# Two scans of a gated recurrence: which of a VectorE instruction's semaphore waits is named first

## The reference, cut to what matters

```
h1_new = tanh(h1 * (1 - alpha) + sigmoid(h1 @ Wh.T + z_t @ Wz.T + b) * z_t)
```

```
z  = sigmoid(xz_t + h @ U_z + vz)
r  = sigmoid(xr_t + h @ U_r + vr)
hh = tanh(xh_t + r * h @ U + vh)
h_new = (1.0 - z) * h + z * hh
```

## Time and profile before

| | |
|---|---|
| median of 3 runs | 3118.3 us (3117.98 to 3118.93) |
| profiled execution | 3121.06 us, its span 3119.7 us |
| busy in the span | PE 88%, PEld 71%, DVE 66%, ACT 52%, POOL 11% |
| stretch with layer 2's steps | 187 to 2283 us, 1024 steps, 2096 / 1024 = 2.05 us each |
| L1765 and L1747 | 1024 and 1023 instructions, 183 ns each |
| EVENT_SEMAPHORE L1764 | 1024, median 50 ns; L1746: 1023, 21 ns each |

### The profile page before, as it was taken

The page is one execution under the profiler, slowest core; times in us unless marked ns, Lnnn a source line. Parts: engine busy times, 40 slices in busy tenths (PEclk is TensorE's granted clock), DMA queues, the critical chain, the costliest instruction groups (busy, mean ns, idle before and its releaser), DMA issues.

```text
span 3119.7 us, 149803 instructions
## 1 busy us (share of the span) xinstructions
PE 2751.6 (88%) x59217; PEld 2221.1 (71%) x59220; DVE 2045.6 (66%) x12108; ACT 1609.6 (52%) x8443; POOL 341.2 (11%) x457
## 2 busy tenths in 40 slices
PE   7689899999999999899999989988659999979984
PEld 4478888888888888788888878877636666644331
DVE  6688888766776666766667665655447666666238
ACT  3445555566666666666666655543325555521115
POOL 0000101101010010100101001010114444410000
PEclk7555555555555555555555555555559999989997
DMA  3142323223122231222312220000457766242000
GB/s 126 41 122 79 96 70 93 62 64 92 49 84 75 66 103 49 83 71 72 94 59 83 63 79 17 4 17 5 170 188 241 218 194 198 86 146 84 0 0 27
DMA packets 170138, 270.88 MB, mean 87 GB/s; under 512 B 23353, under 2 KB 125644, under 8 KB 167140
## 3 DMA queue, kind: packets, MB, share of 16 engines
q1 hardware_dynamic: 125524, 202.29, 20.6%
q0 software_dynamic: 15312, 33.67, 3.2%
q10 hardware_dynamic: 28608, 25.35, 3.0%
HBM read 170.77 MB, written 98.70 MB: 86 GB/s over the span
## 4 chain that ended last, share of the span: by engine, by line
PE 77%; DVE 10%; ACT 5%; issue 5%; DMA 1%; DVEq 1%; SPq 0%; POOL 0%; POOLq 0%; ACTq 0%
PE bank_h L676 7%; PE bank_h L685 7%; PE bank_z L676 7%; PE bank_r L676 6%; PE work L676 6%; PE bank_g L676 5%; PE work L666 5%; PE bank_r L685 3%; DVE h_run L1765 3%; PE bank_z L685 3%; ACT hh_run L1208 3%; PE work L898 3%; PE bank_z L898 3%; PE work L923 2%; PE bank_g L685 2%
## 5 line engine op out<-in xcount | busy, mean ns | idle before, releaser
L676 PEld LDWEIGHTS work<-h_run,hi_r 128*128 128x128 f16 x4092 | 212.7, 109 | 323.6 <-DVE h_run L1765 312.9
L676 PE MATMUL work<-h_run,hi_r 128*128 128x2 f16 x4092 | 277.7, 172 | 169.7 <-DVE h_run L1765 162.7
L1765 DVE TENSOR_TENSOR_SCAN h_run<-z_run,hh_run 128x12 f16<-128x12 f32 x1024 | 187.1, 183 | 326.1 <-ACT hh_run L1208 281.4
L1208 ACT ACTIVATE hh_run<-bank_h 128x4 f32<-128x4 f32 x1024 | 180.1, 176 | 349.2 <-PE bank_h L685 348.9
L1747 DVE TENSOR_TENSOR_SCAN rh_run<-r_run,h_run 128x12 f16<-128x12 f32 x1023 | 186.9, 183 | 213.1 <-ACT r_run L1198 198.7
L1189 ACT ACTIVATE r_guess<-work 128x4 f32<-128x4 f32 x1023 | 177.0, 173 | 286.1 <-PE work L676 274.0
L676 PE MATMUL bank_g<-h_hi,hi_g 128*128 128x2 f16 x4092 | 253.0, 166 | 38.8 <-ACT h_hi L1178 37.0
L685 PE MATMUL bank_h<-rh_run,hi_h 128*128 128x2 f16 x4092 | 270.9, 170 | 10.2 <-DVE rh_run L1747 3.7
L676 PE MATMUL bank_h<-h_run,hi_h 128*128 128x2 f16 x4092 | 256.8, 167 | 3.2 <-DVE h_run L1744 0.5
L685 PE MATMUL bank_g<-h_lo,hi_g 128*128 128x2 f16 x4092 | 252.7, 166 | 4.3 <-issue 2.8
L685 PE MATMUL bank_r<-h_run,hi_r 128*128 128x2 f16 x4092 | 251.5, 165 | 2.4 <-DVE h_run L1781 0.5
(11 more groups left out here) (481 smaller groups left out, 7780.4 us busy)
## 6 DMA issues: line engine op xcount, KB each, us to landing
stage<-in_gate_up SPq DMA_DIRECT2D x128, 384.0 KB, 3.7
stage<-in_down SPq DMA_DIRECT2D x128, 192.0 KB
gu_split<-parts SPq DMA_DIRECT2D x64, 384.0 KB, 2.7
gu_ring<-gu_split SPq DMA_DIRECT2D x64, 384.0 KB
xt<-x_rows ACTq DMA_DIRECT2D x191, 128.5 KB, 2.2
x_rows<-zero_rows SPq DMA_DIRECT2D x64, 257.0 KB, 3.3
yk<-y_rows SPq DMA_DIRECT2D x16, 1024.0 KB, 4.7
dn_split<-parts SPq DMA_DIRECT2D x64, 192.0 KB, 2.7
```

Of the source, the lines that this page charges most:

```text
L676: ins = pe.matmul(o[:, m, step, :], w[:, k, m * P:(m + 1) * P], hi(k), start=False, stop=False, skip_group_check=True)
L1208: act.activation(two(t.hh_run[:, :, 1]), gate_in(t.h, c2, s2), ACT.Tanh, scale=scale_of["h"]).then_inc(s.hh_act, 1)
L1765: dve.tensor_tensor_scan(t.h2_run[:, 0:3 * KH * B], threes(t.z_run), threes(t.hh_run), 0.0, ALU.mult, ALU.add).then_inc(s.h2hi, 1)
```

## The change

On VectorE the order in which the waits in front of two scans are named is changed. L1747 named `rhhi` and then `r_act`; now `r_act` comes first. L1765 (now L1766) named `z_act`, in some steps `h2c`, then `keep` and `hh_act`; now `hh_act` comes first, then `z_act`, `keep` and `h2c`. In a tick in which a bank is filled between (`fill_at(tau, "K")`, 16 of them) `z_act` is waited for in front of the fill as before. No instruction is added, removed or moved, and every wait is still there.

```diff
--- before.py
+++ after.py
@@ -1742,8 +1742,8 @@
                 h_prev = t.h2[(t2 - 1) // STEPS % 2][:, (t2 - 1) % STEPS, :, 2]
                 dve.wait_ge(s.rg_act, t2)
                 dve.scalar_tensor_tensor(t.rh_hi, t.r_guess, -1.0, h_prev, ALU.mult, ALU.mult).then_inc(s.rhhi, 1)
+                dve.wait_ge(s.r_act, t2)
                 dve.wait_ge(s.rhhi, t2)
-                dve.wait_ge(s.r_act, t2)
                 dve.tensor_tensor_scan(threes(t.rh_run), threes(t.r_run), t.h2_run[:, 2:2 + 3 * KH * B], 0.0, ALU.mult,
                                        ALU.subtract).then_inc(s.rhlo, 1)
                 dve.tensor_copy(t.hh_run[:, :, 0::2], h_prev.unsqueeze(2).to_broadcast([P, KH * B, 2])).then_inc(s.keep, 1)
@@ -1752,16 +1752,17 @@
         elif tau == T:
             finish_first(T - 1)
         place_b(tau)
-        if t2 is not None:
-            dve.wait_ge(s.z_act, t2 + 1)
         if fill_at(tau, "K"):
+            if t2 is not None:
+                dve.wait_ge(s.z_act, t2 + 1)
             fill(*fill_at(tau, "K"))
         if t2 is not None:
+            dve.wait_ge(s.hh_act, t2 + 1)
+            dve.wait_ge(s.z_act, t2 + 1)
+            if t2 > 0:
+                dve.wait_ge(s.keep, t2)
             if s2 == 0 and c2 >= 2:
                 dve.wait_ge(s.h2c, c2 - 1)
-            if t2 > 0:
-                dve.wait_ge(s.keep, t2)
-            dve.wait_ge(s.hh_act, t2 + 1)
             dve.tensor_tensor_scan(t.h2_run[:, 0:3 * KH * B], threes(t.z_run), threes(t.hh_run), 0.0, ALU.mult,
                                    ALU.add).then_inc(s.h2hi, 1)
             dve.tensor_tensor_scan(threes(h_new2), threes(t.z_run), threes(t.hh_run), 0.0, ALU.mult,
```

## The result

The changed kernel takes 3006.9 us (median of 4 runs, 3005.3 to 3007.8) against 3118.6 for the kernel before on the same chip (3118.0 to 3120.4): 0.964 of its time, interval 0.9624 to 0.9657, some 112 us less. The forecast was 2989 with 2955 to 3040 around it, so the time lies inside, 18 us above the point (and inside 2970 to 3010, the forecast's own range). The profiled span fell from 3119.7 to 3004.5 us.

A forecast was written before the change was run, and what follows sets the result against it. A chain between engines, with both scans on it, was taken to set each layer 2 step. The terms 77 + 72 - 17 - 3 = 129 us off 3121.1, less 2.8, gave 2989 us, with a stated range of 2955 to 3040.

The forecast's parts named there:

- Which sites are on the path: Scans L1765 and L1747 in layer 2's steps: both on the path, saving 77 - 17 = 60 and 69 us.
- The gap at hh, 0.13 to 0.03: Scan L1765 behind hh: with hh's wait on the scan, the gap shrinks by 0.10 us.
- only 773 steps count: L1765: 0.10 us counts only where TensorE's first weight load waited for this scan, 773 of 1023 steps: 77 us.
- The 250 steps bound by TensorE: Steps where TensorE was still busy when h_new's high part came: no gain from the earlier L1765.
- h's low part: L1781 behind layer 1's scan, in L1684 ticks: late for bank_r's low loads, 242 x 0.07 = 17 us given back.
- The gap at r, 0.10 to 0.03: Scan L1747 behind r_run: 0.07 us saved in all 1023 steps, 72 us.
- 24 x (0.07 + 0.07) = 3 us back: L1747 in 24 steps where bank_h's high products waited for L1744: it gains nothing and pays 0.07 more.
- the tie: bank_h's last loads: due at 1510.56, ready in TensorE's order at 1510.55, so all of the 0.07 us is used.
- One site only: Rival: one of the two scan sites pays, the other not; about 3054 us; chance 0.10.
- nothing: Rival: the gap is the scan's own, from its three-part operands, so time stays 3118 us; chance 0.05.
- the bigger gain: Rival: the 250 steps gain too (+25) and h's low part costs nothing (+17): 2947 us; chance 0.04.
- The slower one: Rival at L1744 to L1747: separate wait for VectorE's own semaphore starts L1747 late; 3242 us at 0.40; chance 0.03.

The follow-up runs named there:

- hh alone: Kernel before with only the scan that makes h_run naming hh_act first, L1747's waits in the old order: 3064.2 us, ratio 0.9826.
- r alone: Kernel before with only L1747's waits in the new order, r_act first and rhhi in the separate wait: 3058.0 us, ratio 0.9802.

## Why the prediction held, and where its sum was off

**Which sites are on the path.** Right. Each alone saves 6 and 8 us less than it was said to, and the savings add.

**The gap at hh, 0.13 to 0.03.** Right: the medians are 130 and 33 ns, and the piece from hh_run to the scan is 101 us shorter with both sites and with hh alone.

**That only 773 steps count.** Nearly right in the sum, wrong in its parts. The forecast had 77 - 17 = 60; hh alone gave 56.6 in the steps of its trace. Step by step against the kernel before, the 773 steps gain 76 us at the scan, as said. The 250 steps bound by TensorE gain 6.8 and not nothing. h's low part costs 9.6, not 17: the low loads wait for L1782 in 146 steps and not in 242. Two costs stand in no term of the sum. In 71 steps TensorE's own order has become the bound, 7 us. And in 74 steps, 7 us go behind a piece of ScalarE's own work in front of r_guess, which does not come earlier when the scan does, as this timeline of the kernel after shows (start us, us); 2 us more are spread. That the errors nearly cancel is luck.

```profile
1246.15 0.29 PEld L676 LDWEIGHTS work<-h_run,hi_r 128*128 128x128 f16 x4 [0.19 <-DVE h_run L1766]
...
1246.48 0.47 ACT L1107 ACTIVATE sig<-work,tok_gate 128x256 f32<-128x256 f32 x1 [0.28 <-PE work L728]
...
1246.85 0.17 ACT L1189 ACTIVATE r_guess<-work 128x4 f32<-128x4 f32 x1
```

r_guess starts 0.70 behind the step's first load, where the ordinary step above has 0.36. ScalarE is in L1107, which waited for a product of its own on TensorE (L728). In the trace of the kernel before the same pieces stand there; in these steps r_guess started 0.49 behind the first load (median) and now starts 0.59 behind.

**The gap at r, 0.10 to 0.03.** The size of the gap is right (101 to 33 ns). The count of steps in which `rhhi` is late is wrong: "24 x (0.07 + 0.07) = 3 us back". The 24 were read from TensorE's wait for L1744, but what counts is whether L1744 ends less than 0.07 us before r does, or later, and that was so in 155 steps of the trace of the kernel before already. It holds the scan back in 146 steps with r alone and in 242 with both. This step of the kernel after is such a one (timeline):

```profile
1248.56 0.48 DVE L1542 SCALAR_TENSOR_TENSOR hmid<-work,tok_up,sig 128x256 f32<-128x256 f32 x1
...
1248.96 0.16 DVE L1744 SCALAR_TENSOR_TENSOR h_run<-r_guess,h 128x4 f16<-128x4 f32 x1
1248.97 0.18 ACT L1198 ACTIVATE r_run<-bank_r 128x4 f32<-128x4 f32 x1
...
1249.23 0.18 DVE L1747 TENSOR_TENSOR_SCAN rh_run<-r_run,h_run 128x12 f16<-128x12 f32 x1
```

r_run ends at 1249.15 and L1744 at 1249.12, 0.03 earlier, so the scan goes by L1744 and starts 0.11 behind it. Most of these steps lose little, since both ends lie close together: with r alone the piece from r_run to L1747 gained 65.9 where 0.068 x 1023 = 69.6 were possible, 3.7 less. So that term of 3 us came out by luck; with both sites it is 5.9. What was mis-sized is the tie. The forecast had TensorE ready at 1510.55 for loads due at 1510.56 and gave nothing back for it, but from L1747 to bank_h's low loads 5.5 us are lost, nearly all in 200 steps in which these loads follow TensorE's load in front at its own pace of 0.027 us (63 steps before). 0.07 for 0.068 makes another 2, and 59.5 were measured in the steps.

**What is late next.** L1782 in the L1684 steps is as forecast in kind, 0.07 in the step shown. Taking it away brought 4 us, since `rhhi` stands right behind it.

**The rivals.** "One site only" falls to the two runs with one site each; "nothing" to the gaps; the bigger gain to the pieces given back. The slower one had the right place and the wrong price: the separate wait for VectorE's own semaphore costs 0.10, not 0.28 or more.

**The sum.** 129 forecast, 112 measured: the two terms' errors, 6 and 8 us with one site each, make most of the 18 us between forecast and time. By size they are: two costs that the sum put at nothing (14 us, with hh alone), the tie at bank_h's low loads (5.5), the gap read as 0.07 (2), and against them 7 us each for the 250 steps and for h's low part.

The section of the Trainium skill weighed there ("VectorE: DVE Perf Modes", The DRAIN you can't avoid) says that eight copies took the same time with a semaphore behind each as with one behind the last. No run here repeats that case, and it does not carry over to this one. Where VectorE is ready and the semaphore comes last, the gap in front of the scan shrinks by 68 and 97 ns when that wait moves onto it.

## What to carry to other kernels

Count only the steps in which that wait is the last on the path, and then ask in each of them what comes within the saved time behind it; most of what lay between 129 and 114 us is of that kind. Where one instruction has two late operands, look at how far apart they arrive in every step, not at who waited longest.

## What the runs showed of the hardware that was not expected

A separate wait costs the same when the semaphore comes from VectorE's own previous instruction: 101 to 105 ns from L1744's end to L1747, though both are on one engine and follow one another.

The same program took 3118 us on one chip and 3193 on another (2.4% more), with a granted clock of 0.50 for TensorE in the steps of both. The traces of the slower chip show nearly all of it: in 106 to 116 steps, by kernel, r_run starts 0.65 to 0.71 us late on average though TensorE was through, which sums to 70 to 76 us. In the traces of the other chips these two starts are never over 0.65 us apart; 0.31 is usual. The timeline of the kernel before with TensorE's order changed, on the slower chip (bank_r's last loads, and r_run, L1195 there):

```profile
346.17 1.00 POOL L2084 DMA_INDIRECT x_rows<-rows,slot  x1 [3.46 <-DVE rh_run L1744]
...
346.62 0.18 PEld L685 LDWEIGHTS bank_r<-h_run,hi_r 128*128 128x128 f16 x4
...
347.52 0.18 ACT L1195 ACTIVATE r_run<-bank_r 128x4 f32<-128x4 f32 x1 [0.56 <-PE bank_r L685]
```

In an ordinary step 0.30 us lie between the starts of the last two rows (1442.67 and 1442.97 after the change); here it is 0.90. The late steps are no chance ones: GpSimd issues an indirect transfer of rows, as in the first line, in 120 of the steps, and all the late steps but 2 are among these, in the four traces of that chip together. In the traces of the other chips the same 120 transfers leave r_run where it was. The kernel before there:

```profile
346.19 0.99 POOL L2087 DMA_INDIRECT x_rows<-rows,slot  x1 [2.75 <-DVE rh_run L1747]
...
346.63 0.18 PEld L685 LDWEIGHTS bank_r<-h_run,hi_r 128*128 128x128 f16 x4
...
346.94 0.18 ACT L1198 ACTIVATE r_run<-bank_r 128x4 f32<-128x4 f32 x1
```

How the transfer holds up ScalarE, and why on one chip only, stays open: no run took the transfers out. Every ratio here is between kernels that ran on the same chip; the table of pieces and the gains by step set traces side by side that may come from different ones.
